# Sorting edges by type in a graph kernel: one-hots of four tiles from one 16-bit tensor-tensor comparison

## The reference

```python
edge_index = jnp.stack([src, dst])
h = jnp.maximum(_layernorm(x), 0.0)
x = x + relation_layer(h, edge_index, edge_type, weight, bias)
h = jnp.maximum(_layernorm(x), 0.0)
x = x + maxk_layer(h, W_self, W_neigh, src, dst)
```

## Time and profile before

| what | us |
|---|---|
| median of 3 runs | 3504.98 (3495.07 to 3508.95) |
| span of the profiled execution (no other time of it is given) | 3513.6 |
| busy in that span: DVE | 3116.0 |
| busy: PE | 2575.6 |
| busy: POOL | 2453.7 |
| busy: ACT | 2177.4 |

### The profile page before, as it was taken

One profiled execution on the slowest core, in us unless ns is written; L12 is line 12 of the kernel. 1 busy time (PEld: TensorE's weight loads), 2 busy tenths in 40 slices (PEclk: granted clock), 3 DMA queues, 4 the chain that ended last, 5 costly groups with the idle time before them and its releaser, 6 DMA issues.

```text
span 3513.6 us, 64945 instructions
## 1 busy us (share of the span) xinstructions
PE 2575.6 (73%) x10738; PEld 1673.1 (48%) x10739; DVE 3116.0 (89%) x13781; ACT 2177.4 (62%) x6002; POOL 2453.7 (70%) x1732
## 2 busy tenths in 40 slices
PE   2665766767788888888677777777777775777777
PEld 1223655555566666666533333333333332556655
DVE  8998778888899999999789999999999998677777
ACT  3995233333333333333388888888888886777786
POOL 0002886767787777777668888888888885777776
PEclk9998888888899999999888999989899998899899
DMA  9601456667655555555534444444444443999997
GB/s 367 266 0 43 77 114 143 148 142 149 130 105 105 100 104 102 104 102 103 110 133 167 176 175 173 167 167 173 177 175 168 167 169 122 297 290 299 298 304 257
DMA packets 308090, 576.92 MB, mean 164 GB/s; under 512 B 32095, under 2 KB 188034, under 8 KB 307982
## 3 DMA queue, kind: packets, MB, share of 16 engines
q1 hardware_dynamic: 212366, 419.40, 34.7%
q0 software_dynamic: 95616, 156.31, 22.9%
HBM read 316.70 MB, written 258.88 MB: 164 GB/s over the span
## 4 chain that ended last, share of the span: by engine, by line
DVE 48%; issue 23%; PE 10%; DMA 9%; POOL 6%; DVEq 3%; ACT 1%; POOLq 1%; SPq 0%; ACTq 0%
DVE zone_c L1175 7%; DVE w L1175 7%; DVE best L1168 6%; DMA agg<-msg,sidx 5%; PE banks L1566 4%; DMA w<-hs,gidx 3%; PE banks L1466 2%; DVE zone_c L1049 2%; DVE zone_c L1203 2%; DVE zone_c L860 2%; DVE zone_c L1051 2%; DVE zone_c L1053 2%; DVE stats L895 2%; DVE zone_c L862 2%; POOL w L734 2%
## 5 line engine op out<-in xcount | busy, mean ns | idle before, releaser
L1538 PE MATMUL banks<-w,hT 128*128 128x512 f32 x1568 | 798.8, 668 | 199.7 <-ACT hT L1321 195.1
L667 POOL DMA_INDIRECT agg<-msg,sidx x400 | 666.9, 1667 | 202.5 <-issue 112.5
L655 POOL DMA_INDIRECT rows_in<-in_x,gidx x400 | 423.4, 1058 | 435.3 <-DVE gidx L911 305.2
L1538 PEld LDWEIGHTS banks<-w,hT 128*128 128x128 f32 x1568 | 327.1, 214 | 615.2 <-issue 503.0
L1203 DVE SCALAR_TENSOR_TENSOR zone_c<-banks,rdeg,zone_c 128x256 f32 x784 | 379.4, 484 | 155.0 <-PE banks L1566 109.7
L1408 PE MATMUL banks<-pick,h 128*128 128x128 f32 x1600 | 289.8, 310 | 309.5 <-ACT h L1220 221.2
L1566 PE MATMUL banks<-w,zone_c 128*128 x1568 | 404.8, 415 | 140.8 <-POOLq L742 105.1
L1466 PE MATMUL banks<-w,hT 128*128 x1600 | 480.9, 428 | 17.5 <-issue 16.2
L734 POOL DMA_INDIRECT w<-hs,gidx x392 | 371.4, 948 | 141.8 <-issue 98.2
L1238 ACT COPY msg<-banks 128x256 f32<-128x256 f32 x400 | 148.2, 370 | 509.9 <-PE banks L1477 489.8
L1408 PEld LDWEIGHTS banks<-pick,h 128*128 128x128 f32 x1600 | 258.7, 217 | 372.5 <-issue 350.0
(11 more groups left out here) (229 smaller groups left out, 5844.4 us busy)
## 6 DMA issues: line engine op xcount, KB each, us to landing
out_rows<-zone_c SPq DMA_DIRECT2D x196, 512.0 KB, 2.7
agg<-bias SPq DMA_DIRECT2D x2, 25344.0 KB, 97.3
zone_c<-agg SPq DMA_DIRECT2D x98, 512.0 KB, 6.0
hs<-zone_c SPq DMA_DIRECT2D x98, 512.0 KB, 3.6
zone_c<-out_rows SPq DMA_DIRECT2D x98, 512.0 KB, 6.2
rows_in<-in_x SPq DMA_DIRECT2D x97, 512.0 KB, 5.3
keyrow<-key_rows SPq DMA_DIRECT2D x100, 320.0 KB, 4.0
zone_c<-bucket_rows SPq DMA_DIRECT2D x28, 448.0 KB
```

The lines of the kernel that those rows point to most:

```text
L655: pool.indirect_dma_start(out=rows_in[p][:, j, :], out_offset=None, in_=x[:, :], in_offset=bass.IndirectOffsetOnAxis(ap=gidx[p][:, j:j + 1 ...
L667: pool.indirect_dma_start(out=agg[:, :], out_offset=bass.IndirectOffsetOnAxis(ap=sidx[p][:, j:j + 1], axis=0), in_=msg[p][:, j * D:(j + 1) ...
L1538: last = mm(bank[4 + j][:, :], hT[p][:, c, j * P:(j + 1) * P], w1[:, c, :], start=(c == 0), stop=(c == KC - 1))
```

## The change

In place of 4 x (one_src, one_dst) and 2 + 2 one_tile made column by column, the one-hots of the four columns of a batch are made together, with the column number j innermost: [rows, 4] and [400, 4]. `iota4` [128, 400, 4] in f16 holds each number four times; the four columns' values of a field are read as a row of four again and again. One comparison gives the rows (`one_row`), one the slot tiles, and two multiplications of one_row with the codes give one_src and one_dst. ACT has no part in it any more. PE reads both of its operands with a step of four elements (8 bytes). The fields are kept in f16 as well (`fields16`).

```diff
@@ sizes
+        iota4 = sb("iota4", [P, SLOTS, B], F16)
+        iota4_i = view(zone_a, STEPS1, [SLOTS, B], I32)
+        fields16 = sb("fields16", [P, FIELDS, COLS], F16)
-        one_src = two_views(zone_c, 0, [B, P], F16)
-        one_dst = two_views(zone_c, B * P, [B, P], F16)
-        one_tile = two_views(zone_c, 2 * B * P, [B, SLOTS], F16)
-        fields4 = two("fields4", [P, B, FIELDS])
+        one_src = two_views(zone_c, 0, [P, B], F16)
+        one_dst = two_views(zone_c, B * P, [P, B], F16)
+        one_tile = two_views(zone_c, 2 * B * P, [SLOTS, B], F16)
+        one_row = two_views(zone_c, 2 * B * P + B * SLOTS, [P, B], F16)
@@ POOL, ahead of the iota that DVE waits for
+            nc.gpsimd.iota(iota4_i[:, :, :], pattern=[[1, SLOTS], [0, B]], base=0, channel_multiplier=0)
             nc.gpsimd.iota(iota_i[:, :], pattern=[[1, STEPS1]], base=0, channel_multiplier=0).then_inc(consts, 1)
@@ DVE, tables
             v.tensor_copy(iota_h[:, :], iota_i[:, 0:COLS])
+            v.tensor_copy(iota4[:, :, :], iota4_i[:, :, :])
...
                 link(v.scalar_tensor_tensor(code16[:, :], tab[n][:, :], float(CODE), tmp_f[:, :], ALU.add, ALU.add))
+                v.tensor_copy(fields16[:, code, :], code16[:, :].bitcast(F16))
                 link(v.tensor_copy(field(code), code16[:, :].bitcast(F16)))
...
             slots_of_positions()
+            v.tensor_copy(fields16[:, SLOT_ROW, :], field(SLOT_ROW))
+            link(v.tensor_copy(fields16[:, SLOT_TILE, :], field(SLOT_TILE)))
@@ DVE, one_hots
                 wait_from(dve, hot_used, b - 1, b, 2)
-                wait_from(dve, slot_near, b - 1, b, 2)
-                v.tensor_copy(fields4[p][:, :, :], fields[:, bass.ds(b * B, B), :]).then_inc(fields_done, 1)
-                dve.wait_ge(fields_done, b + 1)
-                for j in range(B):
-                    f = [fields4[p][:, j, k:k + 1] for k in range(FIELDS)]
-                    v.tensor_scalar(one_src[p][:, j, :], iota_h[:, 0:P], f[SLOT_ROW], f[SRC_CODE], ALU.is_equal,
-                                    ALU.mult)
-                    last = v.tensor_scalar(one_dst[p][:, j, :], iota_h[:, 0:P], f[SLOT_ROW], f[DST_CODE], ALU.is_equal,
-                                           ALU.mult)
-                    if j < B // 2:
-                        v.tensor_scalar(one_tile[p][:, j, :], iota_h[:, 0:SLOTS], f[SLOT_TILE], None, ALU.is_equal)
-                last.then_inc(hot, 1)
+
+                def of(k, n):
+                    return fields16[:, k, bass.ds(b * B, B)].unsqueeze(1).to_broadcast([P, n, B])
+
+                v.tensor_tensor(one_row[p], iota4[:, 0:P, :], of(SLOT_ROW, P), ALU.is_equal).then_inc(row_hot, 1)
+                v.tensor_tensor(one_tile[p], iota4[:, :, :], of(SLOT_TILE, SLOTS), ALU.is_equal)
+                dve.wait_ge(row_hot, b + 1)
+                v.tensor_tensor(one_src[p], one_row[p], of(SRC_CODE, P), ALU.mult)
+                v.tensor_tensor(one_dst[p], one_row[p], of(DST_CODE, P), ALU.mult).then_inc(hot, 1)
@@ ACT: slot_hots (L1256 to L1271) and its pipeline are removed
@@ PE, collect
                 pe.wait_ge(hot, b + 1)
-                pe.wait_ge(slot_hot, b + 1)
...
                     for k, rows in enumerate((one_src, one_dst)):
-                        last = mm(bank[k][:, 0:SLOTS], rows[p][:, j, :], one_tile[p][:, j, :], start=first, stop=final)
+                        last = mm(bank[k][:, 0:SLOTS], rows[p][:, :, j], one_tile[p][:, :, j], start=first, stop=final)
```

More of the change, by code:

```diff
@@ L279, in graph_layers @@
         act_junk = sb("act_junk", [P, B, D])
-        near_slot = act_junk[:, :, :].rearrange("p j d -> p (j d)").bitcast(F16).rearrange(
-            "p (j d) -> p j d", j=B)[:, :, 0:SLOTS]
         best = sb("best", [P, B, 8])
@@ L376, in graph_layers @@
         rank_rows_stored = sem("rank_rows_stored")
-        fields_done = sem("fields_done")
+        row_hot = sem("row_hot")
         hot = sem("hot")
         hot_used = sem("hot_used")
-        slot_near = sem("slot_near")
-        slot_hot = sem("slot_hot")
         keyT_done = sem("keyT_done")
@@ L1254, in edge0_step @@
                 edge0_evict(b, p, 3)
[L1256 to L1271, removed]
             edge0_front(0, 0)
```

## The result

The changed kernel is **slower**, by 1.6%: 3560.95 us median (3557.07 to 3563.64, 4 runs) against 3501.93 (4 runs), ratio 1.0159, 95% interval 1.0144 to 1.0174. On another chip it was 3559.91 against 3504.74, ratio 1.015 (1.0133 to 1.0168). I had forecast 3456, and 3512 was the top of the range.

What follows compares the result with a forecast made beforehand. DVE was taken to bound the type sort: 52.9 us gone there, less 4.0 us added ahead, net 48.9. From the median, 3504.98 - 48.9 = 3456 us, 1.4% faster, range 3436 to 3512.

Steps and rivals of the forecast that it cites:

- PE's side: PE in the sort: stepped reads of both operands cost nothing, so DVE stays the bound, by 0.08 us only.
- The prediction's own sign of being wrong: New profile of the sort: DVE shows waits for PE in every batch, meaning the stepped read costs.
- DVE's four instructions: DVE in each sort batch: four two-source instructions at two elements a cycle, 1.89 us, 1.91 with the loop.
- PE's matmuls: PE in each sort batch: the eight matmuls of 400 columns stay at 1.51 us, 0.167 each.
- PE's stepped read becomes the bound: L1383 to L1385: at half rate, 0.334 us a matmul, sort 22 us longer, 3532 us in all; chance 0.10.
- Ahead of the sort: Before the sort: POOL's iota, its cast and four field copies add 4.0 us, bounds 3.3 and 6.
- Behind the sort: From the decode on: nothing the gain can run into, all moves forward as one by the net 48.9 us.
- The base of the sum: Whole kernel: gain taken from the 3504.98 us median of three runs, 8.6 us under the profile's 3513.6 span.

Runs made afterwards that it cites:

- experiment 1: Kernel before plus eight series of matmuls ahead of its first collect, with operands dense or read with various steps; one run, 3618.41 us.
- 2: Changed kernel with rows made column by column and dense, so only PE's moving operand is stepped; 3689.12 us against 3617.51, ratio 1.0198.
- experiment 3: Changed kernel with dense tile one-hots (three by DVE, one by ACT), so only PE's stationary operand is stepped; 3559.35 us against 3617.51, ratio 0.9843.
- 6: Changed kernel with tiles compared two columns at a time (moving step of 4 bytes) and tables made by DVE; 3579.65 us against 3620.39, ratio 0.9884.
- 4: Kernel before with nine more dense matmuls a batch into an unused bank; 3667.86 us against 3617.51, ratio 1.0151.
- the tables: Kernel before with all the change adds ahead of the sort (POOL's iota, cast, 16-bit fields), sort untouched; 3515.31 us against 3504.74, ratio 1.0031.
- table on DVE: Changed kernel with its table made by one DVE copy in place of POOL's iota and the cast; 3544.02 us against 3504.74, ratio 1.0104.
- experiment 7: Changed kernel with three one-hots written column by column by DVE with a stepped target, so PE reads dense; 4525.92 us against 3620.39, ratio 1.25.
- experiment 8: Kernel of experiment 3 with GpSimd making one tile, DVE two and ACT one; 3572.44 us against 3620.39, ratio 0.9868.
- 9: Kernel of experiment 3 with a batch's two products in one instruction of 1024 elements; 3446.21 us against 3508.56, ratio 0.9824.

## Why the prediction was wrong

The step that failed stands in "PE's side": "I take no cost for PE". A matmul whose moving operand is read with a step of 8 bytes takes 0.355 us, not 0.167, and PE's batch 2.845 us, not 1.51. That is longer than the 2.461 us of the old batch, and 98 times the difference, 38 us, is what the sort grew by. The prediction's own sign of being wrong came: DVE waits for PE in 96 of 98 batches. Shown by experiment 1 (the step alone), 2 (that operand alone), 3 (the other operand alone, and the time falls) and 6 (half the step, and the loss is gone). My reason for no cost was that the step and the elements are smaller than in L841's cast; that compared a target of DVE with a source of PE and was no measurement of either. The rule that I let weigh there, the Trainium skill's "SBUF — State Buffer", in the part on the DMA port swizzle, with two accesses in a 16-byte line at full rate, doesn't hold for this read: the line has two, and the rate is less than half (0.352 us against 0.169, experiment 1).

Term by term:
- **DVE's four instructions**: right. Two elements a cycle; 0.985 us for the tiles (0.98 forecast), 0.42 for the others. The Trainium skill, "Vector Engine (DVE) Microarchitecture Reference", §5.1, agrees: the row of four read again and again kept two a cycle.
- **PE's matmuls**: wrong, as said. The rival "PE's stepped read becomes the bound" named the mechanism, the place and the sign, at 0.10; its price of 0.334 was an even half rate, taken from no row, and that it came so near is luck. 0.355 adds 98 x (2.845 - 2.69) = 15 us to its 27. The prediction also misread the page that it set beside this rival: the figures of the Trainium skill, "Vector Engine (DVE) Microarchitecture Reference", §5.2, are 1.71 to 2.51 ns a column against 1.05, so 1.6 to 2.4 times, not 1.7 to 2.5; PE's step of 8 bytes cost 2.1 times.
- **Ahead of the sort**: 7.2 us, not 4.0, and beyond my upper bound of 6. POOL's iota took 4.7 us, not 1.4. I had priced it by the slope of L651, 0.82 ns a number; the pattern that holds each number four times ran at 2.89 ns, (4.76 - 0.13) / 1600. The cast (0.9) and the copies (1.6) were right within 0.1.
- **Behind the sort**: that a change of the sort passes on to the end holds roughly. With the experiment in brackets, the decode's shift and the change in time were -58 and -58 (3), +53 and +50 (4), +7 and +11 (the tables), +40 and +39 (table on DVE), +66 and +72 (2), -44 and -41 (6), +900 and +906 (7), -53 and -48 (8), -62 and -62 (9), and in the single run of 1 +9 and +1. The changed kernel has the widest gap: 44.9 against 59 and 55. So 10 to 14 us of its loss stay open. They aren't the sort's: two profiles of each kernel have the decode within 0.3 us of each other. Nor does a profile show them. From the decode to the end the two profiles of before took 3210.4 and 3196.8 us, the two of the change 3207.3 and 3202.2, and these two are of executions 4 and 8 us faster than their median. The edge stage took 1464 to 1478 us and the merge stage 534 to 545 (on those chips) across all these kernels with no order that I can see.

The base of the sum did no harm: the profile of before was of an execution some 12 us above the median, and the sum starts from the median (3504.98, and 3501.93 with the fourth run).

## What to carry to other kernels

Before a layout is changed to suit DVE's two elements a cycle, price the other reader: a step in the moving operand is paid per column of every matmul, and here 8 bytes cost more than the change won. The gain was to be had by splitting the change: the new layout for the stationary operand, whose load hides, and dense for the moving one. And freeing an engine that is off the path (ACT with half of the tiles) bought nothing here; the two fastest kernels kept it for one tile in four. What they would take without it wasn't tried.

## What the runs showed of the hardware

- In experiment 1 PE's matmul of 400 f16 columns took 0.169 us with a dense moving operand, 0.177 with a step of 4 bytes, 0.352 with 8 and 0.704 with 16. The three stepped ones have one pace in bytes: 0.44, 0.88 and 1.76 ns a column, some 9.1 bytes a nanosecond. A stepped stationary operand of 128 columns stayed hidden (eight matmuls in 1.54 us against 1.51, experiment 3).
- In experiment 1 PE's granted clock fell from 1.00 to 0.50 while it ran matmuls without a pause, those with a moving step of 16 bytes, and the series with the stepped stationary operand behind them ran at that clock (0.331 us a matmul).
- DVE's two-source 16-bit instructions with a target step of 256 and 800 bytes cost 4.9 and 4.2 ns an element in experiment 7 ((2.66 - 0.15) / 512, (6.83 - 0.15) / 1600), against the 1.7 times that a 16-byte step cost a cast in the earlier trace rows.
- A one-source copy on DVE that repeats one element four times kept two a cycle (1600 in 0.99 us), where the two-source comparison with an element repeated 98 times is at one.
- GpSimd's iota with each number four times took 2.89 ns an element against 0.82 for a plain one, 3.5 times; whether the repeat or the second dimension of the pattern costs it wasn't tried. Beside GpSimd's tile in experiment 8 DVE's one-source comparisons of 400 columns took 463 ns, and 320 without it.
